# Attention kernel: one layout of the maxima units over all head groups, and a later load of the third group

## The reference

```python
q, k, v = (layernorm(x) @ W.T split into heads, for W in (Wq, Wk, Wv))
logits = einsum('bhqd,bhkd->bhqk', q, k) * DH ** -0.5        # 1024 x 1024 for each of 8 x 16 heads
logits = where(causal_mask, -max, logits)
e = exp(logits - max(logits, axis=-1))                        # the row maximum is subtracted
out = einsum('bhqk,bhkd->bhqd', e / sum(e), v)
x = x + out @ Wo.T
```

## Time and profile before

| | us |
|---|---|
| three runs | 2202.27, 2201.95, 2199.97 (median 2201.95) |
| the profiled execution | 2202.19, its span 2200.2 |
| PE busy | 2041.9 (93% of the span) |
| DVE busy | 1906.2 (87%) |
| ACT busy | 1287.6 (59%) |
| mean granted clock of PE | 0.965 of full speed |
| attention: first unit to the last group's values | 689.9 to 1659 |

### The profile page before, as it was taken

One profiled execution on the slowest core, in us unless ns is written; L12 is line 12 of the kernel. 1 busy time (PEld: TensorE's weight loads), 2 busy tenths in 40 slices (PEclk: granted clock), 3 DMA queues, 4 the chain that ended last, 5 costly groups with the idle time before them and its releaser, 6 DMA issues. The chain is left out here.

```text
span 2200.2 us, 44394 instructions
## 1 busy us (share of the span) xinstructions
PE 2041.9 (93%) x13448; PEld 1335.3 (61%) x13448; DVE 1906.2 (87%) x4327; ACT 1287.6 (59%) x2221; POOL 1037.8 (47%) x1639
## 2 busy tenths in 40 slices
PE   4799999997999799999999999999996799999998
PEld 3688888886885233333333333333335688888887
DVE  6799999996987789898888888898853699999996
ACT  3455555542763477777777777777783345555553
POOL 4788888883655011111111111111110388888884
PEclk9899999997997799999999999999998999999998
DMA  6000000001689477777777777877624100000000
GB/s 213 1 1 0 0 0 0 0 0 38 226 237 208 54 120 138 133 128 132 131 131 131 123 131 133 137 124 134 120 79 155 48 15 19 19 19 19 19 20 25
DMA packets 163502, 184.91 MB, mean 84 GB/s; under 512 B 57696, under 2 KB 109280, under 8 KB 163040
## 3 DMA queue, kind: packets, MB, share of 16 engines
q1 hardware_dynamic: 160672, 182.11, 39.6%
q10 hardware_dynamic: 2688, 1.05, 0.2%
HBM read 113.90 MB, written 85.98 MB: 91 GB/s over the span
## 5 line engine op out<-in xcount | busy, mean ns | idle before, releaser
L1476 POOL TENSOR_SCALAR_AFFINE_SELECT diag_scores<-diag_scores 128x256 f32<-128x256 f32 (+1 forms) x192 | 94.5, 493 | 581.4 <-ACT diag_scores L1439 577.5
L1512 DVE CUSTOM_DVE_ANT_0 gu_ps<-gu_ps,mask_qk 128x256 f32<-128x256 f32 x511 | 291.7, 597 | 73.7 <-PE gu_ps L1299 71.7
L1441 ACT ACTIVATE probs<-hT_ps 128x512 f32<-128x512 f32 (+3 forms) x320 | 273.7, 855 | 133.4 <-PE hT_ps L1321 75.9
L1299 PE MATMUL gu_ps<-k_stack,q_stack 96*128 96x512 bf16 (+3 forms) x994 | 319.2, 349 | 21.0 <-DVE part_max L1512 8.6
L721 PE MATMUL gu_ps<-wguT_hi,ffn_xT_hi 128*128 128x512 f32 (+1 forms) x768 | 313.1, 408 | 7.3 <-DVE ffn_xT_lo L597 5.1
L1340 PE MATMUL gu_ps<-probs,v_group 128*17 128x512 f32 (+3 forms) x3072 | 312.5, 494 | 2.2 <-ACT probs L1441 1.1
L721 PE MATMUL gu_ps<-wguT_hi,ffn_xT_lo 128*128 128x512 f32 (+1 forms) x768 | 290.2, 378 | 0.0
L721 PE MATMUL gu_ps<-wguT_lo,ffn_xT_hi 128*128 128x512 f32 (+1 forms) x768 | 289.8, 377 | 0.0
L699 ACT ACTIVATE ffn_z<-xs,ffn_shift,ffn_rstd 128x256 f32 (+1 forms) x128 | 77.1, 602 | 349.5 <-POOL ffn_shift L650 349.5
L1441 ACT ACTIVATE probs<-av_ps 128x512 f32<-128x512 f32 (+3 forms) x320 | 275.3, 860 | 0.6 <-PE av_ps L1321 0.5
L1299 PEld LDWEIGHTS gu_ps<-k_stack,q_stack 96*128 96x128 bf16 x994 | 91.8, 98 | 294.6 <-DVE part_max L1512 157.7
(11 more groups left out here) (211 smaller groups left out, 5120.0 us busy)
## 6 DMA issues: line engine op xcount, KB each, us to landing
q_stack<-q_parts SPq DMA_DIRECT2D x192, 128.0 KB, 7.0
k_stack<-k_parts SPq DMA_DIRECT2D x192, 128.0 KB, 7.6
o_all<-o_sb SPq DMA_DIRECT2D x64, 256.0 KB
q_parts<-qkv_parts SPq DMA_DIRECT2D x32, 384.0 KB, 2.7
k_parts<-qkv_parts SPq DMA_DIRECT2D x32, 384.0 KB, 2.8
v_ones<-qkv_vst SPq DMA_DIRECT2D x16, 544.0 KB, 3.8
v_group<-v_ones SPq DMA_DIRECT2D x32, 272.0 KB, 11.0
xs<-in_L_attn_x SPq DMA_DIRECT2D x8, 1024.0 KB, 12.0
```

The lines of the kernel that those rows point to most:

```text
L1299: mm = T.matmul(out[:, e, :], qs[0:STACK, h0 + e, t * P:(t + 1) * P], ks[0:STACK, h0 + e, c * CHUNK:c * CHUNK + w], start=True, stop=True)
L1441: S.activation(probs[:, pair, i % 2, :, first:w], scores[pair][:, :, first:w], ACT.Exp, scale=DH ** -0.5).then_inc(s[pr], 1)
L1476: G.affine_select(out=block_of, in_=block_of, compare_op=ALU.is_ge, fill=MASKED, base=0, pattern=[[0, 2], [0, count], [1, P]], channel_mul ...
L1512: last = V.tensor_tensor_reduce(out=ps[:, e * w:(e + 1) * w], in0=ps[:, e * w:(e + 1) * w], in1=mask_qk[:, CHUNK - w:CHUNK], scale=1.0, sc ...
```

## The change

One list of entries is laid out over all 32 groups, and each engine looks up its entries by group, step and part.

- 44 units stand in front of group 0's first score: 38 of group 0 and 6 of group 1.
- From there the units go in at 1.06 times the rate of the steps until the layout is one and a half groups ahead, which is in group 5; from group 6 on each step holds the same units as before the change. In groups 0 to 5 a group holds 40 or 41 units instead of 38.
- The transposition of a group's maxima follows directly behind u2 of the next group (`TURN_AT`), in the same slot, and no longer behind the values and u3. For the groups from 6 on this is step 5, part 3. In groups 0 to 4 it is step 8 part 0, step 7 part 3, step 7 part 0, step 6 part 3, step 6 part 0. The last one, for group 31, follows behind the last unit, in group 30, step 4, part 4.
- On DVE `m_lo` comes behind u4 of the next group (`LOW_AT`), as before from group 5 on.
- On ACT `m_hi` follows the exponential of the pair in whose part the transposition stands. `store_max` comes two steps after it (one step where two would leave the group), `load_max` three steps after it or at the end of the group. In groups 0, 1 and 2 the load stands behind the group's last step; in groups 3 and 4 ahead of step 9.
- SP waits for the first maxima to be loaded before it issues the loads of groups 2 and 3.
- `loaded` is waited for just ahead of a group's first unit.

```diff
+            BANKS = 3
+            HEAD, HASTE, AHEAD = 6, 1.06, 1.5
+            TURN_AT, LOW_AT = 2, 4
+            ENTRIES, entries_in, turned_in = [], {}, {}
+            def units_until(n, i):
+                at = n + sum(widths[:i]) / sum(widths)
+                if n < 0:
+                    return 0
+                return min(round(NU * min(AHEAD + at, 1 + HEAD / NU + HASTE * at)), NU * NG)
...
+                for _ in range(count):
+                    k = sum(what[0] == "unit" for what in ENTRIES)
+                    add("unit", k // NU, k % NU)
+                    if k // NU and k % NU == TURN_AT:
+                        add("turn", k // NU - 1)
+                        turned_in[k // NU - 1] = i, min(part // 2, 1)
+                    if k == NU * NG - 1:
+                        add("turn", NG - 1)
+                        turned_in[NG - 1] = i, min(part // 2, 1)
+            enter(-1, 0, 0, units_until(0, 0))
+            for n in range(NG):
+                for i in range(NS):
+                    for part, count in enumerate(SLOTS[units_until(n, i + 1) - units_until(n, i)]):
+                        enter(n, i, part, count)
+            def store_step(n):
+                t = turned_in[n][0]
+                return t + 2 if t + 2 < NS else t + 1
...
-            turned = list(range(MAX_STEP, NS)) + list(range(MAX_STEP))
-                units_of[i] = [(2 if i >= MAX_STEP else 1, u) for u in range(first, round(NU * seen / sum(widths)))]
-                    if i == MAX_STEP and part == 4:
-                        plan[i].append(("entry", enter(("turn_max",))))
-            FIRST = ([("unit", 0, u) for u in range(NU)] + [("unit", 1, u) for u in range(2)] + [("turn_max", 0)]
-                     + [("unit", 1, u) for u in range(2, EARLY)])
...
                         qkv_stored(sp)
+                        sp.wait_ge(max_loaded[0], 16)
                         fill(sp, 0, 2)
...
+                        def max_entry(e):
+                            if e >= BANKS:
+                                kind, n, *which = ENTRIES[e - BANKS]
+                                if kind == "unit":
+                                    once(pe, "reduced", n * NU, which[0] + 1)
+                                else:
+                                    once(pe, "m_lo", n, 1)
+                            kind, n, *which = ENTRIES[e]
+                            of = n // GROUPS, n % GROUPS
+                            if kind == "turn":
+                                turn_max(*of, max_bank(e))
+                            else:
+                                if which[0] == 0:
+                                    loaded(pe, *of)
+                                max_unit(*of, which[0], max_bank(e))
...
                             for i, w in enumerate(widths):
-                                if i == MAX_STEP + 2 and nxt:
+                                if nxt and i == store_step(n + 1):
                                     store_max(*nxt)
-                                if i == MAX_STEP + 3 and nxt:
+                                if nxt and i == turned_in[n + 1][0] + 3:
                                     load_max(*nxt)
...
+                                    if nxt and (i, pair) == turned_in[n + 1]:
+                                        m_hi(*nxt, max_bank(turn_entry[n + 1]))
...
-                                if i == MAX_STEP and nxt:
-                                    m_hi(*nxt, max_bank)
+                            if nxt and store_step(n + 1) == NS:
+                                store_max(*nxt)
+                            if nxt and turned_in[n + 1][0] + 3 >= NS:
+                                load_max(*nxt)
...
+                            reduce_unit(*of, which[0], max_bank(e))
+                            if which[0] == NU - 1:
+                                finish_max(*of)
+                            if which[0] == LOW_AT and n:
+                                m_lo((n - 1) // GROUPS, (n - 1) % GROUPS, max_bank(turn_entry[n - 1]))
+                            if which[0] == NU - 1 and of == LAST:
+                                m_lo(*LAST, max_bank(turn_entry[n]))
```

More of the change, by code:

```diff
@@ new lines, in attention @@
+            enter(-1, 0, 0, units_until(0, 0))
[6 more added lines that the diff above has]
+                return t + 2 if t + 2 < NS else t + 1
+            turn_entry = {what[1]: e for e, what in enumerate(ENTRIES) if what[0] == "turn"}
+            MAX_STEP = 5
@@ L1344, in values @@
                             mm.then_inc(s["pv"], 1)
-                        loaded(pe, 0, 0)
-                        for e, (kind, g, *which) in enumerate(FIRST):
-                            if e >= BANKS:
-                                kind_before, g_before, *which_before = FIRST[e - BANKS]
-                                if kind_before == "unit":
-                                    once(pe, "reduced", g_before * NU, which_before[0] + 1)
-                                else:
-                                    once(pe, "m_lo", g_before, 1)
-                            if kind == "unit":
-                                if g and which[0] == 0:
-                                    loaded(pe, 0, g)
-                                max_unit(0, g, *which, turn_ps[e % BANKS])
-                            else:
-                                turn_max(0, g, turn_ps[e % BANKS])
+                        for e in entries_in[-1, 0, 0]:
+                            max_entry(e)
@@ L1360, in _ @@
                         pe.wait_ge(s["filled"], RING)
                         def group(b, g, last):
-                            prev = before(b, g)
+                            n, prev = b * GROUPS + g, before(b, g)
                             pe.wait_ge(max_loaded[g % RING], b * 16 + 16)
                             for i in range(NS):
-                                if i == MAX_STEP and later(b, g, 2, last):
-                                    loaded(pe, *later(b, g, 2, last))
-                                for what, at in plan[i]:
-                                    if what == "part" and at < 4:
-                                        score_head(b, g, i, at // 2, at % 2)
-                                    elif what == "part" and i:
+                                for part in range(5):
+                                    if part < 4:
+                                        score_head(b, g, i, part // 2, part % 2)
+                                    elif i:
@@ L1543, in group @@
+                        for e in entries_in[-1, 0, 0]:
+                            max_entry(e)
                         def group(b, g, last):
-                            prev, nxt = before(b, g), later(b, g, 1, last)
+                            n, prev = b * GROUPS + g, before(b, g)
                             for i in range(NS):
-                                units = [(later(b, g, ahead, last), u, turn_ps[bank_of["unit", ahead, u]])
-                                         for ahead, u in units_of[i] if later(b, g, ahead, last)]
-                                if i == MAX_STEP and nxt:
-                                    finish_max(*nxt)
-                                for of, u, ps in units[:1]:
-                                    reduce_unit(*of, u, ps)
-                                if i == MAX_STEP + 1 and nxt:
-                                    m_lo(*nxt, max_bank)
-                                for of, u, ps in units[1:]:
-                                    reduce_unit(*of, u, ps)
+                                for part in range(5):
+                                    for e in entries_in[n, i, part]:
+                                        max_entry(e)
```

80 lines of the change are left out of this document (19 added, 61 removed).

## The result

The changed kernel takes 2222.28 us (median of 6 runs, 2218.36 to 2224.11) against 2199.44 for the kernel before on the same chip (6 runs): ratio 1.0100, 95% interval 1.0087 to 1.0113. It is slower, by about 22.8 us in the medians; forecast were 2218 and a range of 2204 to 2236, as a loss of 16.1 us.

What follows compares the result with a forecast made beforehand. PE was taken to bound the groups, except for six microseconds at the turn, where DVE's chain does. Terms -12.8 + 2.9 + 17.3 + 1.0 + 1.3 + 5.0 + 1.4 = +16.1 us on 2202.2 gave 2218, range 2204 to 2236.

Steps and rivals of the forecast that it cites:

- Front, -12.8: Before group 0's first score: fewer units and a quick store and load of the first maxima gain 12.8 us.
- Turn, 0.69 a group: Groups 5 to 29: with the transposition ahead of the values, u5 waits for m_lo, losing 0.69 us a group.
- The free turn: First rival: PE's smaller waits take up the delay at the transposition, so it costs nothing; 2200 us, chance 0.16.
- Its total, 16.6 in 24 groups: The turn's loss of 0.69 us taken over the 24 groups from group 5's copy to group 29's.
- The others I leave as they are: Clock term: one more fall at group 1's start, a loss of 1.4 us; the existing falls were left unchanged.
- First groups, 11.0 forecast: First score to group 5's copy: moved units 2.9, early turns 1.0, maxima loads 5.0, clock 1.4, group 5's first piece 0.7.
- The waits at the starts of groups 1, 2, 3: PE waits for maxima loaded at the previous group's end: a loss of 5.0 us, ends 3.1 and 13.
- 2.9 + 1.0 + 0.7: Loss in us from 13 units moved into groups 0 to 5, turns of groups 0 to 4, group 5's first piece.
- the odd turns: Turns in groups 0 to 4, with other neighbours: a loss of 1.0 us for the five, between 0 and 3.5.
- The last turn, 1.3: Transposition right behind the last u37: PE waits for the row maxima, a loss of 1.3 us once.
- The clock falling at each turn: Second rival: PE's longer waits at the turn bring 22 more clock falls, 30 us, so 2248; chance 0.10.
- The collision of the late loads with group 1's maxima: Third rival: group 1's store takes 12.4 us behind the late loads, PE waits 13.6 longer, 2232; chance 0.12.

Runs made afterwards that it cites:

- e4: The kernel before plus one line: SP waits for the first maxima to be loaded before the loads of groups 2 and 3; 2193.02 us, ratio 0.9967.
- e5: The changed kernel without SP's wait, so the loads of groups 2 and 3 are issued as before; 2232.35 us, ratio 1.0160.
- e1: The changed kernel with the transposition one unit later, behind u3 (TURN_AT 3 in place of 2); 2208.0 us, ratio 1.0030.
- e2: The changed kernel with m_lo one unit earlier on DVE (LOW_AT 3 in place of 4), transposition left behind u2; 2210.76 us, ratio 1.0049.
- e11: The kernel before with SP's sends of each group's first half issued ahead of the output stores; 2194.83 us, ratio 0.9976 to the kernel before.
- e10: The changed kernel with transposition and m_lo behind u3, 44 units in front and the 13 others all in group 0; 2191.97 us, ratio 0.9964.
- e3: The changed kernel with 57 units in front of the first score, as before the change (HEAD 19 in place of 6); 2212.14 us, ratio 1.0056.
- e6: The changed kernel with the maxima of groups 2 and 3 stored one step earlier and loaded ahead of step 9; 2217.46 us, ratio 1.0093.
- e7: The changed kernel with 57 units in front and both transposition and m_lo behind u3; 2186.34 us, ratio 0.9948 to the kernel before.
- e9: e7 with SP, in group 0, sending the first half, then waiting for group 1's maxima before group 3's loads; 2196.21 us, ratio 0.9984.

## Why the prediction was right

The sign, the time and the main steps held: 2222.28 against 2218, and 19.0 against 16.1 between the profiled executions. The loss in the medians, 22.8, is 6.7 more than forecast; the time comes nearer than that because the kernel before's median over six executions is 2199.44, and the forecast started from 2202. And two errors of opposite sign, 7.7 and 6.7 us, stand in the sum, so that its closeness is partly luck.

**Front, -12.8: right.** Measured -13.4. Each link is within 0.6 us: counted from the first unit, `m_lo` was forecast at 29.8 and came at 29.81, the store at 30.1 and came at 30.11, the load at 31.6 and came at 31.58, the first score at 34.1 and came at 33.53. The load took 1.95 and not 2.4. e4 and e5 show that neither half of the change gives it alone.

The Trainium skill (DMA: Bandwidth & Descriptors, "Anatomy of one DMA") gives a transfer a fixed cost of about 2.0 us, in a section on transfers issued from GpSimd; these two are issued from ACT. The trace has 1.4 to 1.5 for the store when the queues are quiet and 1.95 for the load; the measurement decides, and the term was the better for going by it. What mattered was the other end of the same row: 12.7 for this store in e5, and 5.4 for that of group 1 in e4, when group loads are in flight.

**Turn, 0.69 a group: right in mechanism, 0.77 in size.** The transposition waited for u0, the values started at 3.27 behind u37 (forecast 3.19), u5 came 0.33 behind `m_lo` at 6.07 (5.98), the next values at 6.94 (6.86), and nothing later took it back. The missing 0.08 is `m_lo`, which is 0.16 later than before and not "within 0.1". e1 undoes the loss by the place alone, e2 divides it. The free turn, the first rival, fell with that.

**Its total, 16.6 in 24 groups: 18.5 came, and 8.6 went back.** Two steps failed: the sentence on the clock, "The others I leave as they are", and behind it the assumption that one group costs the same as the next. Three groups of the kernel before hold a fall of the clock, 4.1 us, and the kernel after's execution has none. The forecast took nothing from the 13 groups in which DVE waits for the sums, 5.1 us; after the change three such groups carry 0.2. (Of these 9.0 us 0.4 are used up in other groups of the kernel after.) The waits come from a second chain beside PE's: SP sends an output half, loads the sums, waits for DVE's reciprocal, spreads it, sends the next half. e11 shows without any change of the turn that this chain costs time: the order of SP's sends alone takes 3.1 of the 5.1 away. That a group longer by 0.77 us gives the chain the time it lacks is read from the table of periods: at 29.05 and 29.57 few waits are left. But the chain has no fixed length of its own: at 28.61 the mean group is 28.8 to 29.0 us long, and at 28.80, with SP's old order, 29.1 to 29.2. What sets its length isn't shown, nor whether the falls went because of the change; e4 lacks them too.

**First groups, 11.0 forecast, 18.7 came: mis-sized in three terms.** The waits at the starts of groups 1, 2, 3 were forecast at 2.6, 1.2 and 1.2 and are 3.04, 1.14 and 3.09 (7.3 for 5.0). Group 3's is the large error: its load was issued at 821.61 and released PE at 825.79, 4.2 us, where 1.4 to 2.4 was taken; why that load was slow isn't shown. (The upper end given for this term, 13, adds up to 13.9: twice 4.2, and 5.5 in group 0.) The clock fell twice and not once; by the granted clock these falls take at most 4.5 us for 1.4. The remaining 7.0 belong to the 13 units and to the turns, for which 2.9 + 1.0 + 0.7 was forecast. They can't be parted cleanly. PE's waits around the six turns of this part sum to 10.3 after and 4.9 before, so the turns took up to 4.9 more than before beside group 5's, not 1.0: the three behind part 0, which I took as about free, hold 1.9, 1.1 and 1.1 us of waits (0.86 before), and the two behind part 3 hold 2.3 and, with a wait of 0.5 nine microseconds on, 2.7. On the other side, e10's 0.45 a unit would make the 13 units 5.9. Against e3 it is 0.3 (181.46 and 167.49, less the visible waits of 17.6 and 12.2 and the clock's 4.5, are some 4.1 apart). Either way the bounds given (2.9 to 9.0, 0 to 3.5) were better than the values chosen: at PE's price for the units and at nothing for the odd turns, I took the low end twice.

**The last turn, 1.3: right,** with this line of the timeline after:

```profile
1644.29 0.27 PE L1315 MATMUL xd_ps<-ident,row_max 128*32 128x128 f32 x1 [1.30 <-DVE row_max L1518]
```

The stretch around it, to the end of the span, came out at +2.6; the rest of that was not looked into.

**The rivals.** The free turn is refuted by e1 and e2. The clock falling at each turn is refuted by the 24 groups at 1.00: pieces of 1.14 and 0.87 us, three microseconds apart, did not bring one fall. In the first groups, where the piece ahead of the transposition can be 1.32, a fall followed directly on one of two such pieces in e2, e5 and e6, and on neither in the kernel after. The Trainium skill's rule (TensorE: Matmul & The Clock Gate, "What's actually happening"), by which activity releases a throttled clock, was read as saying that more idle time in a turn brings more falls; in the 24 groups the trace went the other way, with more idle time in every turn and fewer falls. The front, which was named as agreeing, shows 0.50 with PE busy 32.00 of 38.80 us, and so says nothing of what releases the clock. The collision of the late loads with group 1's maxima is real but was smaller than the 12.4 feared: 5.4 us from the store's issue to the load's in e4, 7.7 in e7, and 2.8 in the changed kernel, where the store is issued later.

## What to carry over

Before an instruction is moved in a round of three buffers, write down who stands three places behind it as well as ahead: here one place earlier put u5 instead of u6 behind `m_lo`, and that is worth 0.5 us in each group. Look at the spread of a loop's period and not only at its most frequent value: groups that take 0.2 to 1.4 us longer now and then point to a second chain that sometimes ends last, or to the clock, and what a slower main loop costs is then partly given back. And a large load that is made to wait doesn't go away; ask what will stand behind it next (the store of group 1's maxima in e4 and e7, the sends of the output in e9).

## What the runs showed of the hardware that was not expected

A store of 16 KB took 1.4 to 1.5 us with quiet queues, 2.2 to 7.7 where the held-back loads of other groups were in flight or just ending (group 1's store, and 4.8 for group 2's in e9), and 12.4 to 12.7 with the loads of three groups in full course. A fall of PE's clock from 2.4 to 1.2 GHz came in the kernel before in a stretch without a long idle time: 0.57 over 901 to 905, and in the turn ahead of it PE waited 0.16, 0.44 and 0.26 us. It came so 3 times in the 24 groups of the kernel before, once in e1 and not in e4, whose turns are the same, nor in the 24 groups in which each turn held 2.01 us of waits (the kernel after, e3, e5, e6). At single waits of 2.2 to 4.7 us in the first groups it came each time (the kernel after, e1, e2, e5, e6, e7, e9), behind one of two waits of 1.32 in e2, e5 and e6, behind neither in the kernel after, and not at waits of 1.4 to 1.9 (e1, e4, e5). What brings a fall behind the short waits is open: no run was made on it by itself.
